# Another order of the items on all four engines between the first and the second attention of a two-layer adaLN kernel

## The reference

```
mod = silu(c) @ wmod -> sa, ca, ga, sb, cb, gb
h = layernorm(x) * (1 + ca) + sa
x = x + ga * attention(h)
h = layernorm(x) * (1 + cb) + sb
x = x + gb * ffn(h)
```

## Time and profile before

| | us |
|---|---|
| median of 3 runs | 2210.58 |
| lowest and highest of them | 2207.31, 2214.37 |
| the profiled execution, its own time | 2213.3 |
| its span in the trace | 2211.2 |
| busy: PE, DVE, ACT, POOL | 2153.0, 1702.5, 1461.9, 1225.7 |

### The profile page before, as it was taken

The page is one execution under the profiler, slowest core; times in us unless marked ns, Lnnn a source line. Parts: engine busy times, 40 slices in busy tenths (PEclk is TensorE's granted clock), DMA queues, the critical chain, the costliest instruction groups (busy, mean ns, idle before and its releaser), DMA issues.

```text
span 2211.2 us, 41636 instructions
## 1 busy us (share of the span) xinstructions
PE 2153.0 (97%) x11084; PEld 1653.9 (75%) x11084; DVE 1702.5 (77%) x3418; ACT 1461.9 (66%) x2868; POOL 1225.7 (55%) x1086
## 2 busy tenths in 40 slices
PE   7999999999999989999999999999999999999978
PEld 4888888888887657777777777777777777777655
DVE  6777677777777668888888888888888877788755
ACT  2444444444444668888888888888888877777732
POOL 4656665665663446666666666666666621455332
PEclk9999999999999999999999999999999999999998
DMA  7010010010004142111111111111111112343241
GB/s 244 20 48 29 19 47 28 19 47 28 19 14 125 36 175 83 48 43 48 47 48 42 48 48 46 49 42 49 47 48 42 48 49 59 105 120 90 80 126 39
DMA packets 125622, 132.46 MB, mean 60 GB/s; under 512 B 33277, under 2 KB 75805, under 8 KB 125548
## 3 DMA queue, kind: packets, MB, share of 16 engines
q1 hardware_dynamic: 121708, 118.97, 18.1%
q0 software_dynamic: 3840, 12.59, 1.9%
HBM read 101.59 MB, written 29.36 MB: 59 GB/s over the span
## 4 chain that ended last, share of the span: by engine, by line
PE 92%; DVE 4%; ACT 1%; DMA 1%; issue 1%; POOL 1%; SPq 0%; POOLq 0%; DVEq 0%; ACTq 0%
PE bank L2379 12%; PE bank L2386 11%; PE bank L2366 11%; PE bank L1951 9%; PE bank L1953 9%; PE bank L1952 9%; PE bank L2407 6%; PE bank L2298 5%; PE bank L2297 5%; PE bank L2296 5%; PE bank L2404 2%; PE bank L2087 2%; DVE rope_b L1479 1%; DVE rope_b L1480 1%; DVE rope_a L1478 1%
## 5 line engine op out<-in xcount | busy, mean ns | idle before, releaser
L1761 DVE TENSOR_REDUCE mcol<-bank 128x1 fp32r<-128x512 f32 x1024 | 694.2, 689 | 222.7 <-PE bank L2366 212.8
L2379 PE MATMUL bank<-q,k 128*128 128x512 f32 x1024 | 419.3, 410 | 2.0 <-DMA k<-kc_d 2.0
L2366 PE MATMUL bank<-km,q 128*128 128x512 f32 x1024 | 404.8, 396 | 3.2 <-DVE mcol L1761 1.6
L2386 PE MATMUL bank<-q,k 128*128 128x512 f32 x1024 | 407.0, 397 | 0.0
L2366 PEld LDWEIGHTS bank<-km,q 128*128 128x128 f32 x1024 | 316.3, 309 | 51.4 <-DVE mcol L1761 4.2
L1282 ACT ACTIVATE pT<-bank 128x512 f32<-128x512 f32 x512 | 284.9, 599 | 81.4 <-PE bank L2386 77.6
L1282 ACT ACTIVATE x<-bank 128x512 f32<-128x512 f32 x512 | 284.7, 600 | 80.7 <-PE bank L2386 77.1
L2379 PEld LDWEIGHTS bank<-q,k 128*128 128x128 f32 x1024 | 192.4, 188 | 128.9 <-ACT x L1282 44.3
L2386 PEld LDWEIGHTS bank<-q,k 128*128 128x128 f32 x1024 | 192.5, 188 | 32.4
L2298 PE MATMUL bank<-hT_hi,wr_lo 128*128 128x512 f32 x512 | 202.9, 396 | 0.0
L2296 PE MATMUL bank<-hT_hi,wr_hi 128*128 128x512 f32 x512 | 200.7, 392 | 1.6 <-DVE k L1634 1.6
(11 more groups left out here) (344 smaller groups left out, 5041.5 us busy)
## 6 DMA issues: line engine op xcount, KB each, us to landing
wst<-in_L_attn_Wq_rope SPq DMA_DIRECT2D x64, 256.0 KB, 3.0
o_d<-ost SPq DMA_DIRECT2D x512, 32.0 KB, 1.8
st_q<-in_L_attn_wq SPq DMA_DIRECT2D x8, 1024.0 KB, 7.8
st_wo<-in_L_attn_wo SPq DMA_DIRECT2D x8, 1024.0 KB, 5.2
km<-kc_d SPq DMA_DIRECT2D x256, 32.0 KB
q<-qc_d SPq DMA_DIRECT2D x256, 32.0 KB
k<-kc_d SPq DMA_DIRECT2D x256, 32.0 KB
wm<-in_L_wmod SPq DMA_DIRECT2D x6, 1024.0 KB, 10.5
```

Of the source, the lines that this page charges most:

```text
L1761: dve.tensor_reduce(mcol[:, k % 2, i % 4, i // 4:i // 4 + 1], bank[4 + i % 2][:], AX.X, ALU.max, negate=True)\
L2366: pe.matmul(bank[4 + i % 2][:], q2[:, k % 4, h, i % 4:S:4], km[:, b, h], start=True, stop=True).then_inc(max_mm, 1)
L2379: pe.matmul(bank[s % 4][:], k1[:, k % 2, t], q1[:, k % 4, h], start=True, stop=False)
L2386: pe.matmul(bank[s % 4][:], k2[:, k % 2, h, t], q2[:, k % 4, h], start=False, stop=True).then_inc(scores1, 1)
```

## The change

The change writes the calls of the passage in another order on PE, ACT, DVE and POOL. No call is added or removed, and no shape, buffer or bank changes. SP's program is the same. A follower of the code should know that two ACT table loads (an ACT instruction that the compiler puts where Exp and Sqrt alternate) disappear, because `norm_std(1, 0)` now stands behind the last `exps`.

The diff, cut to its core:

```diff
 (GpSimd)
             add_ffn(0)
+            norm(1, 1)
             add_ffn(1)
-            norm(1, 1)
...
-            add_ffn(4)
             split_latent_weights()
             norm(2, 0)
+            add_ffn(4)
             add_ffn(5)
             add_ffn(6)
             add_ffn(7)
-            split_rope_weights(0, 0)
             zero_others()
             norm(2, 1)
+            split_rope_weights(0, 0)
 (ScalarE)
-            norm_std(1, 0)
             merged_high(0)
             weights_high(4 * LAST + 1, 1)
+            out_high(4 * LAST)
             merged_high(1)
+            exps(4 * LAST + 2, 2)
+            merged_high(2)
             exps(4 * LAST + 3, 3)
-            merged_high(2)
             merged_high(3)
             out_high(4 * LAST + 1)
+            weights_high(4 * LAST + 2, 2)
             gates(0, 1, gate_f0)
-            weights_high(4 * LAST + 2, 2)
+            norm_std(1, 0)
...
-            clear_queries(0)
             norm(1, 1)
             mod_rows(1, (5,))
-            clear_queries(1)
             latent_weights_high()
             norm_std(2, 0)
+            clear_queries(0)
             mod_rows(1, (4,))
+            clear_queries(1)
+            norm(2, 0)
             clear_keys(0)
-            norm(2, 0)
             clear_keys(1)
             latent(0)
-            content_high(0, (0,))
             value_columns(0)
             norm_std(2, 1)
+            content_high(0, (0,))
+            norm(2, 1)
             keys(0)
-            norm(2, 1)
             latent(1)
 (VectorE)
+            gate_attention(4 * LAST, 1)
+            norm_stats(1, 0)
             weights_low(4 * LAST + 2, 2)
             normalise(4 * LAST + 3, 3)
+            norm_rows(1, 0)
+            out_low(4 * LAST + 2)
             gate_attention(4 * LAST + 1, 1)
-            out_low(4 * LAST + 2)
             mod_cols(1, 0)
...
             norm_rows(2, 0)
             ffn_out(4)
+            ffn_out(5)
             norm_split(2, 0, (0, 1))
             mod_scale_late()
-            ffn_out(5)
             norm_split(2, 0, (2, 3))
+            clamp_gates(1)
             ffn_out(6)
-            clamp_gates(1)
             ffn_out(7)
             norm_stats(2, 1)
             split_rope_weights(0, 0, 0)
             norm_rows(2, 1)
+            norm_split(2, 1, (4, 5))
+            norm_split(2, 1, (6, 7))
             content_low(0, (0,))
             key_low(0)
-            norm_split(2, 1, (4, 5))
-            norm_split(2, 1, (6, 7))
             content_low(0, (1,))
 (TensorE)
-            scores(4 * LAST + 1, LAST, 1, 1)
             transposes(4 * LAST, 0)
             merge_factors()
             merge_turn(0)
             merge_turn(1)
+            scores(4 * LAST + 1, LAST, 1, 1)
+            merge(0)
...
-            mod(1, 5)
             norm(1, 1)
             ffn(2)
+            mod_use(1, 2)
+            mod(1, 5)
             ffn(3)
-            mod_use(1, 2)
-            mod(1, 4)
             mod_use(1, 5)
             ffn(4)
+            mod(1, 4)
+            ffn(5)
+            norm(2, 0)
             mod_use(1, 4)
-            norm(2, 0)
-            ffn(5)
             ffn(6)
             ffn(7)
             latent(0)
             content(0, (0,))
             value_columns(0)
+            norm(2, 1)
             keys(0)
-            norm(2, 1)
+            latent_and_keys(1)
             rope_queries(0, 0, 0, range(KT), True, True)
-            latent_and_keys(1)
```

More of the change, by code:

```diff
@@ L1185, in content_high @@
                         act.activation(c_full[:, i], bank[i][:], ACT.Copy).then_inc(c_hi_done, 1)
-            weights_high(4 * LAST, 0)
             merged_turned(0)
             merged_turned(1)
+            weights_high(4 * LAST, 0)
             exps(4 * LAST + 1, 1)
-            exps(4 * LAST + 2, 2)
-            out_high(4 * LAST)
-            norm_std(1, 0)
             merged_high(0)
             weights_high(4 * LAST + 1, 1)
+            out_high(4 * LAST)
             merged_high(1)
+            exps(4 * LAST + 2, 2)
+            merged_high(2)
             exps(4 * LAST + 3, 3)
-            merged_high(2)
             merged_high(3)
             out_high(4 * LAST + 1)
+            weights_high(4 * LAST + 2, 2)
             gates(0, 1, gate_f0)
-            weights_high(4 * LAST + 2, 2)
+            norm_std(1, 0)
             mod_rows(1, (0, 1))
@@ L1639, in content_low @@
                     dve.tensor_tensor(c_lo[:, i], bank[i][:], c_hi[:, i].bitcast(F32), ALU.subtract).then_inc(c_split, 1)
-            gate_attention(4 * LAST - 1, 0)
             merged_factors()
+            merged_scaled()
             mask(4 * LAST + 1, 1)
-            merged_scaled()
             weights_low(4 * LAST, 0)
+            normalise(4 * LAST + 1, 1)
+            merged_low(0)
             mask(4 * LAST + 2, 2)
-            normalise(4 * LAST + 1, 1)
-            norm_stats(1, 0)
-            merged_low(0)
             out_low(4 * LAST)
             merged_low(1)
+            gate_attention(4 * LAST - 1, 0)
+            weights_low(4 * LAST + 1, 1)
+            merged_low(2)
             mask(4 * LAST + 3, 3)
             normalise(4 * LAST + 2, 2)
[L1654 to L1657, removed]
             merged_low(3)
             out_low(4 * LAST + 1)
+            gate_attention(4 * LAST, 1)
+            norm_stats(1, 0)
             weights_low(4 * LAST + 2, 2)
             normalise(4 * LAST + 3, 3)
+            norm_rows(1, 0)
+            out_low(4 * LAST + 2)
             gate_attention(4 * LAST + 1, 1)
-            out_low(4 * LAST + 2)
             mod_cols(1, 0)
             weights_low(4 * LAST + 3, 3)
+            norm_stats(1, 1, (0, 1))
             gate_attention(4 * LAST + 2, 1)
+            out_low(4 * LAST + 3)
             norm_split(1, 0, (0, 1))
-            out_low(4 * LAST + 3)
-            norm_stats(1, 1, (0, 1))
             norm_split(1, 0, (2, 3))
             gate_attention(4 * LAST + 3, 1)
-            ffn_out(0)
             norm_stats(1, 1, (2, 3))
             norm_rows(1, 1)
+            ffn_out(0)
+            norm_split(1, 1, (4, 5))
             ffn_out(1)
-            norm_split(1, 1, (4, 5))
             ffn_out(2)
@@ L2306, in _ @@
             merge_turn(1)
+            scores(4 * LAST + 1, LAST, 1, 1)
+            merge(0)
             scores(4 * LAST + 2, LAST, 1, 2)
             sum_values(4 * LAST, LAST, 1, 0)
-            merge(0)
+            merge(1)
+            transposes(4 * LAST + 1, 1)
             scores(4 * LAST + 3, LAST, 1, 3)
-            transposes(4 * LAST + 1, 1)
-            merge(1)
             merge(2)
@@ L2315, in _ @@
             project_out(4 * LAST, HKV - 1)
-            transposes(4 * LAST + 2, 2)
             sum_values(4 * LAST + 1, LAST, 1, 1)
             broadcast_gate(0, 1)
+            transposes(4 * LAST + 2, 2)
             project_out(4 * LAST + 1, HKV - 1)
```

## The result

The changed kernel takes 2215.56 us (median of 20 runs, 2212.36 to 2218.96), the kernel before 2210.88 in the runs beside it. The ratio is 1.0022, with a 95% interval of 1.0016 to 1.0028: 4.7 us slower, where I had forecast 0.7 us faster.

The account below looks back on a forecast made before the run. PE was taken to set the pace, with only its 8.1 us of waiting, plus low-clock loss, movable. Terms -0.4 - 0.8 + 0.4 + 1.6 - 1.2 - 0.7 + 0.4 = -0.7 us gave 2209.9, stated as 2209.8; range 2204 to 2216.

Parts of the forecast that it names:

- To ffn(0): From the passage's start to ffn(0): PE's lead was put at -0.4 us, bounds -0.9 and 0.
- fer: Ahead of ffn(0): PE's 0.3 us wait on fer goes, since it is there in time.
- mod_cols: Ahead of norm_pair(0): DVE's mod_cols(1, 0) ends about 0.4 us after PE arrives, bounds 0 to 0.9.
- The cover named for ACT: Before ffn(0): two vanished table loads shorten ACT but cost nothing, covered by PE's own matmuls.
- To latent(0): From ffn(0) to latent(0): -0.8 us saved, +0.4 for a new wait on norm(2, 0)'s last low part (0 to 0.7).
- modrow: Ahead of mod_use(1, 4): PE's 0.8 us wait on the modulation row goes, fully covered.
- Value columns to the first maxima: Behind the value columns: +1.6 us at norm(2, 1), -1.2 on key_low(0), -0.7 on value column and latent copy.
- The wait on xn: At norm(2, 1), directly behind the value columns: a new PE wait of 1.4 to 2.0 us, taken as +1.6.
- the 0.7 on the latent: Before the first maxima: a little of PE's 0.7 us wait on the latent copy saved, within the -0.7.
- SP's queue: First content store 3.8 us later; +0.4 us at the first maxima, next content store costs nothing.
- rival 3: At the first maxima: landing 1.5 us longer, second unit's loads later too; about +2 us, 2211.9; chance 0.12.
- Rivals 4 and 5: 4: new waits don't appear, 2205.8 to 2207.5, chance 0.18; 5: DVE and POOL overlap in norms, +0.9 to +2.7, chance 0.08.

Follow-up runs that it names:

- e9: Changed kernel with GpSimd's add_ffn(1) ahead of norm(1, 1) again; one run, no median given, 33.29 us from ffn(0) to latent(0).
- e10: Changed kernel with mod(1, 4) on TensorE back directly ahead of mod_use(1, 5); one run, no median given, 34.17 us from ffn(0) to latent(0).
- e1: Changed kernel with content_low(0, (0,)) back ahead of norm_split(2, 1) on VectorE; median 2213.02 us, ratio 1.0020 to the kernel before.
- e11: Changed kernel without its middle part and with content_low(0, (0,)) ahead of norm_split(2, 1); median 2210.28 us, ratio 1.0001 to the kernel before.
- e6: Kernel before with only the part of the change ahead of ffn(0), on all engines; median 2209.27 us, ratio 0.9994.
- e8: Same kernel as e1, run a second time; median 2211.71 us, ratio 1.0004 to the kernel before.
- e2: Kernel before with only the part of the change behind latent(0); median 2215.38 us, ratio 1.0021.
- e4: Changed kernel with content_high(2, (0,)) one period later on ScalarE, behind q_high(1); median 2211.33 us, ratio 1.0010 to the kernel before.
- e12: e11 with norm(2, 0) and mod_use(1, 4) behind ffn(5) on TensorE, norm(2, 0) ahead of clear_keys(0) on ScalarE; 2209.74 us, ratio 0.9998.
- e14: Changed kernel with content_low(0, (0,)) ahead of norm_split(2, 1) and add_ffn(1) ahead of norm(1, 1); 2211.92 us, ratio 1.0009 to the kernel before.

## Why the prediction was wrong

**To ffn(0).** Right: -0.55 against -0.4; fer is gone, no new wait on mod_cols. The cover named for ACT held.

**To latent(0).** Forecast -0.4 for this stretch (0.8 saved on modrow, 0.4 spent), measured +1.64. The 0.8 was saved. The new wait is 1.73 us, with bounds 0 to 0.7: I let the statistics come 0.8 us earlier, and they came later (the square root 22.75 us after ffn(0) instead of 20.72). 1.3 of these 2.0 us are GpSimd's adds behind its low parts and var_eps beside a GpSimd instruction (e9). The other 0.75 us is PE's own work, against "the change cannot shorten PE's own work (it issues the same instructions)": it issues the same, but in four blocks of small matmuls instead of two (e10).

**Value columns to the first maxima.** Forecast +1.6 - 1.2 - 0.7 = -0.3, measured -0.25. The wait on xn is 1.67; the one on key_low(0) went wholly (0.4 left by forecast), that on the value column too, and the 0.7 on the latent stayed.

**SP's queue.** This is the step that failed, in the sentence "The next content is stored with 5 or more us in hand and costs nothing, unless the first one is later than I think." I followed the queue to the first maxima, where the slack of 4.5 to 5 us was right: the first L2366 came at 804.42 with no wait on a transfer. I did not look who waits for the next store to land. That is ACT, and it had no slack there: in the kernel before it went on at 811.53, when the store had just landed (806.91 + 4.5). The store of content 1 was issued 3.4 us later (810.28 for 806.91). ACT's 0.78 us of waiting for the rotary queries took some of that up, so the copy of the queries came 2.6 us later (817.84 for 815.28). PE, whose clock had not fallen at 806 this time, was there 0.9 us earlier, and its wait grew by 3.4 us. The first store itself was also later than I said, 791.05 for 788.9. I put the next store at nothing; the stretch behind it, from the first maxima to the first scores, became 4.7 us longer. This is rival 3's queue ("SP's queue takes the lead away", 0.12, +2 us), but through a buffer that is not free, not through a load, and at twice its price.

**The clock.** Rival 2 put a fall behind the value columns. The changed kernel's trace has none there, but one behind the 4.5 us wait, of 5.1 us of full clock instead of the 1.7 I priced (3.5 of them as busy time of PE, against e1). Rival 2's own fall does come in other executions: the clock fell at the transposes of norm(2, 1) in six of the ten traces with the new order behind the value columns, and in none of the seven with the old order. My reading of the falls before was off as well: the one at 684 us stands behind a wait of PE of 2.04 us (it ends at 682.99), so it is not one "that no long wait explains". The timed runs, which list their mean granted clock, say that the clock was lower in them too: 0.9921 over the 20 runs of the changed kernel, 0.9939 over 120 of the kernel before, which is (1 - 0.9921) * 2214 = 17.5 us lost against 13.4. The means differ by 5.0. The 4.1 us can't be read as a share of that: they count the clock while PE waits, and e11 lost 2.5 us more than the kernel before by the same sum (0.9928) and is no slower.

**Rivals 4 and 5.** Nothing of 4 appeared. 5 did once, on var_eps and not on a low part, 1.0 us.

**Median and noise.** The executions of one kernel spread over 4.9 us (e6) to 15.2 us (e1) in sets of 11 or 12, with reasons outside of the change among them: the first matmul starts at 10.8 to 13.2 us, when its weights have landed, and the falls of the clock at the end of the kernel (2100 to 2200 us) come to 1.7 to 8.5 us. That is why no verdict here rests on one span, and why differences of 2 us stay unclear after 12 runs.

## What to carry to other kernels

When an instruction moves in front of a store, follow the store both ways: to the loads behind it in its queue, and to the engine that waits for the buffer to come free, with everything queued behind that wait. A slack is to be read at each of these from a row; the one that I took from reasoning was the one that was not there. Compare for it the landing of the store with the start of the copy behind it, since the row may name another engine. Copies on which TensorE waits next should not stand in a queue behind a copy that waits for a transfer. And the price of a long wait is not the wait alone: behind the 4.5 us for which TensorE was idle here, a stretch at 1.2 GHz cost it another 3.5 us.

## What the runs showed of the hardware

The granted clock fell in pieces of 1.7, 3.4 or 5.1 us of full clock each in the passage, PE's idle time in them counted (behind the wait of 1.05 us on q none in e1 and e8, behind the 4.5 us 5.1 us). The same waits do not always bring a fall: around the transposes of norm(2, 1), behind the same wait of 1.7 us, the clock fell in e2, e4, e9, e10, e12 and e14 and stayed in the changed kernel, e1, e8 and e11. What decides was not found.

A DVE tensor_scalar of 128x4 took 1.18 us instead of 0.17 where a GpSimd instruction had begun 0.14 us before it, and 0.22 where 0.19 us of one were left; both ended 0.03 us behind that instruction. Matmuls of the form 128*32 between matmuls of 128*128 cost 0.1 to 0.2 us for each switch.

A ScalarE copy into a buffer that a transfer was reading went on 0.1 us after the transfer had landed, which took 3.9 to 4.6 us from issue for 512 KB (before, changed, e1).
